# Normalisation on VectorE tile by tile, with mean and root as scalars, in a four-sublayer transformer kernel on one Trainium2 core

## Chip, core and metric

One NeuronCore of a Trainium2 chip runs the whole kernel in one launch. The metric is the device time of that launch in microseconds (us), as the median of several runs. A profiled execution gives the rows shown below.

## What is computed

The input x is 32 sequences of 32 tokens of 128 features (1024 tokens), in float32. Four sublayers are added to it one after the other: an attention behind a language adapter with a layer norm, a low-rank mixture feed-forward, a stack of eight linear-attention blocks, and a routed tree feed-forward with attention. The change bears on the layer norms: one in the first sublayer and two in each of the eight blocks of the third:

```python
def _ln(x, scale, bias):
    m = jnp.mean(x, axis=-1, keepdims=True)
    v = jnp.var(x, axis=-1, keepdims=True)
    return (x - m) * jax.lax.rsqrt(v + EPS_LN) * scale + bias

for i in range(8):
    residual = x
    Q = fmap(x @ Wq[i] + bq[i]); K = fmap(x @ Wk[i] + bk[i]); value = x @ Wv[i] + bv[i]
    KV = einsum('nsh,nsh->nh', K, value); Ksum = sum(K, axis=1)
    V = Q * KV[:, None, :] * 1.0 / (Q * Ksum[:, None, :] + 1e-6)
    x = _ln(gelu(V @ Wo[i] + bo[i]) + residual, ln1_s[i], ln1_b[i])
    residual = x
    x = _ln(gelu(gelu(x @ W1[i] + b1[i]) @ W2[i] + b2[i]) + residual, ln2_s[i], ln2_b[i])
```

## The kernel before

Each engine has an instruction stream written out by hand, and the engines meet only through semaphores. The 1024 tokens are two halves (h = 0, 1) of 512. A half in token order is one SBUF tile of 128 partitions by 512 columns, which are four 128x128 tiles (`TILES` = 4) side by side: token on the partition, feature along the row. `yt[:, h]` is such a half before the norm and `xn[:, h]` after it.

The norm of one half is made by three pieces:

- `stats` (lines 834 to 844) on VectorE (DVE): for each of the four tiles a `bn_stats` (L837) and a `bn_aggr` (L841) leave mean and variance of every token in `mv[:, h, i, 0]` and `mv[:, h, i, 1]`. L843 adds epsilon into `rv` and raises the semaphore `var`. L844 then subtracts the four means from all 512 columns of `yt` in place.
- `root` (L505, L506) on GpSimd (POOL): waits for `var`, raises the 128x4 values of `rv` to the power -0.5 into `rstd`, and raises the semaphore `rstd`.
- `normalise` (lines 846 to 849) on VectorE: waits until its own earlier instructions are written (`own.sync`, L847) and for `rstd` (L848), multiplies all 512 columns of `yt` by the roots into `xn` (L849), and raises `xn`.

Then TensorE (PE) turns the four tiles of `xn` into feature order (L1230), and scale and bias are applied on the way out of PSUM: for the first norm of a block by ScalarE (ACT, L582, function `affine` there), for the second by VectorE (L1122, into `cf`).

The eight blocks are a software pipeline over the halves. One `segment` takes half `a` of block `l` through its attention part and, interleaved, half `b` of block `m` through its feed-forward part. There are 16 segments for VectorE (the first has no second half, twelve are four to each of three passes of a hardware loop), and a last norm stands alone. The order on VectorE within a segment is written out:

```python
def segment(l, a, sa, m, b, sb_):
    keys(l, a, sa)
    values(l, a)
    norm_sum(l, a, 0)          # L831: yt = attention part + residual
    stats(a, EPS_LN)
    if m is not None:
        norm_sum(m, b, 1)      # L831, for the other half
    norm_scale(l, a, 0)        # normalise
    if m is not None:
        stats(b, EPS_LN)
        norm_scale(m, b, 1)    # normalise
        affine(m, b, sb_)      # L1122
```

So there are 34 norms of a half: 2 in the first sublayer and 32 in the blocks (16 of `a`, 15 of `b` and the last one). TensorE waits for each `xn` in its own fixed order, and fills its known gaps with matmuls on a tile of zeros (`keep_warm`, L1237). Near the end POOL has more to do than roots: `split` (L527, L528) divides 128x1024 weights into two parts, a cast followed by a subtraction. One such pair stands in POOL's stream between the last segment's second root and the last root, others right behind the last root. SyncE (SP) issues the weight loads and waits for nothing that the norm makes.

Of the kernel before, what the change touches and what calls it, by code (L numbers as in the profile page):

```python
# [11 lines left out]
ALU = mybir.AluOpType  # L12
# [4 lines left out]
B, S, D = 32, 32, 128  # L17
# [3 lines left out]
TILES = HT // P  # L21
# [125 lines left out]
def network(nc, I, konst, out):  # L147
    ctx = ExitStack()
    with ctx:
        def sb(name, shape, dt=F32):  # L150
            return ctx.enter_context(nc.sbuf_tensor(name, shape, dt))
# [56 lines left out]
        yt = sb("yt", [P, 2, TILES, D])  # L208
        stat = sb("stat", [P, 2, TILES, 6])
        after_stats = sb("after_stats", [P, 1])  # L210
        mv = sb("mv", [P, 2, TILES, 2])
        rv = sb("rv", [P, 2, TILES])
        rstd = sb("rstd", [P, 2, TILES])
# [15 lines left out]
        with ExitStack() as once:  # L229
            def sb_once(name, shape):  # L230
                return once.enter_context(nc.sbuf_tensor(name, shape, F32))
# [4 lines left out]
            xn = sb_once("xn", [P, 2, TILES, D])  # L236
# [33 lines left out]
        S_ = Sems()  # L270
# [27 lines left out]
        def by_batch(ap):  # L298
            return ap.rearrange("p (b s) -> p b s", s=S)
# [8 lines left out]
        def spread(ap, n):  # L308

            return ap.unsqueeze(len(ap.shape)).to_broadcast([*ap.shape, n])  # L310
# [496 lines left out]
        def _(dve):  # L807
            own = Chain(dve, S_["dve"])
            V = nc.vector
# [23 lines left out]
            def stats(h, eps):  # L833

                own.sync()
                for i in range(TILES):
                    own.step(V.bn_stats(stat[:, h, i, :], yt[:, h, i, :]))  # L837
                own.sync()
                own.step(V.memset(after_stats[:, :], 0.0))
                for i in range(TILES):  # L840
                    own.step(V.bn_aggr(mv[:, h, i, :], stat[:, h, i, :]))  # L841
                own.sync()
                V.tensor_scalar(rv[:, h, :], mv[:, h, :, 1], eps, None, ALU.add).then_inc(S_["var"], 1)  # L843
                own.step(V.tensor_tensor(yt[:, h], yt[:, h], spread(mv[:, h, :, 0], D), ALU.subtract))  # L844

            def normalise(n, h):
                own.sync()  # L847
                dve.wait_ge(S_["rstd"], n)  # L848
                V.tensor_tensor(xn[:, h], yt[:, h], spread(rstd[:, h, :], D), ALU.mult).then_inc(S_["xn"], 1)  # L849


            for c in range(LCH):
# [14 lines left out]
            for h in HALVES:  # L867
                dve.wait_ge(S_["a_out"], h + 1)
                add_residual(h, ps[h][:, 3, :], xt[0][:, h].rearrange("p i d -> p (i d)"))
                stats(h, EPS_COND)  # L870
            for h in HALVES:
                normalise(h + 1, h)
# [13 lines left out]
            for h in HALVES:  # L886
                dve.wait_ge(S_["b_qk"], h + 1)
                qe = z(h, 8, 4).rearrange("p g (b j s) -> p (g b) j s", b=GB, j=HPQ)
                for j in range(HPQ):
                    ins = V.tensor_scalar(qe[:, :, j, :], by_batch(ps[h][:, 0, :]), rope_bias[:, 0:1],  # L890
                                          kc[:, K_HEAD + j:K_HEAD + j + 1], ALU.add, ALU.mult)
# [238 lines left out]
            def norm_scale(l, h, n):  # L1130

                normalise(norm_count(l, h, n) + 2, h)
# [4 lines that stand above are left out]
                norm_sum(l, a, 0)  # L1137
                stats(a, EPS_LN)
                if m is not None:
                    norm_sum(m, b, 1)  # L1140
                norm_scale(l, a, 0)
                if m is not None:
                    stats(b, EPS_LN)
                    norm_scale(m, b, 1)
                    affine(m, b, sb_)
# [59 lines left out]
            for h in HALVES:  # L1205
# [5 lines left out]
                for q in range(P // QUAD):  # L1211
                    rows_q = slice(q * QUAD, (q + 1) * QUAD)
                    pt = z(h, 12).rearrange("p (i n) -> p i n", i=TILES)
                    ins = V.transpose(pt[rows_q, :, rows_q], e[rows_q])
# [551 lines left out]
```

## Time and profile before

| | us |
|---|---|
| median of 3 runs | 737.95 (737.72 to 741.58) |
| the profiled execution | 736.44 |
| its span, first to last instruction | 734.5 |
| PE busy in the span | 656.1 |
| VectorE busy | 441.0 |
| ScalarE busy | 309.5 |
| GpSimd busy | 114.2 |

The 1.94 us between the profiled execution and its span lie around the program. The mean TensorE clock granted over the span was 0.943 of full speed. A busy PE includes the matmuls that only fill gaps. The blocks run from about 235 to 560 us.

### The profile page before, as it was taken

How to read it: one execution, taken by the hardware profiler on the slowest of the kernel's cores; microseconds unless marked ns; L12 is line 12 of the kernel's file. 1: busy time of each engine (PE TensorE's matmuls, PEld its weight loads, DVE VectorE, ACT ScalarE, POOL GpSimd, SP SyncE). 2: the span in 40 equal slices, each digit the busy share in tenths (PEclk: the TensorE clock that was granted, in tenths of full speed). 3: DMA queues.
4: the chain of work that ended last, by engine and by line, in shares of the span. 5: the costliest groups of instructions: out<-in, count | busy, mean ns of one | idle time of the engine just before them, and what ended most of it. 6: DMA issues, size and time to landing. Idle time of an engine off the chain costs nothing.

```text
span 734.5 us, 9622 instructions
## 1 busy us (share of the span) xinstructions
PE 656.1 (89%) x3358; PEld 444.6 (61%) x3379; DVE 441.0 (60%) x1021; ACT 309.5 (42%) x488; POOL 114.2 (16%) x93
## 2 busy tenths in 40 slices
PE   9986899899896689999999999999985999999996
PEld 4655586787684345555555555555554877555595
DVE  5579502557768366766666666676655477743344
ACT  4044203343343355555555555555542432344341
POOL 0030130013210011111111111111132127200000
PEclk9599868999999699999999999999996998999997
DMA  3011587000003000101010101010000000000000
GB/s 84 24 44 48 142 222 174 1 0 1 1 0 124 20 1 5 40 1 44 1 43 0 43 0 43 0 43 0 0 1 0 1 1 0 1 0 1 0 1 30
DMA packets 43726, 21.79 MB, mean 30 GB/s; under 512 B 14627, under 2 KB 40799, under 8 KB 43692
## 3 DMA queue, kind: packets, MB, share of 16 engines
q1 hardware_dynamic: 43692, 21.33, 10.8%
q8 instruction: 21, 0.34, 0.2%
q14 instruction: 13, 0.11, 0.0%
HBM read 20.73 MB, written 0.52 MB: 29 GB/s over the span
## 4 chain that ended last, share of the span: by engine, by line
PE 46%; issue 29%; DVE 16%; POOL 5%; ACT 2%; POOLq 0%; DVEq 0%
PE ps L1503 7%; PE ps L1486 7%; POOL rstd L506 5%; PE ps L1692 5%; PE ps L1710 4%; PE ps L1237 3%; PE ps L1716 2%; DVE z L1017 2%; PE ps L1230 2%; PE ps L1283 2%; DVE zr L1058 2%; PE ps L1364 1%; PE ps L1404 1%; PE ps L1377 1%; PE ps L1570 1%
## 5 line engine op out<-in xcount | busy, mean ns | idle before, releaser
L506 POOL TENSOR_TENSOR rstd<-rv,minus_half 128x4 f32<-128x4 f32 x34 | 46.8, 1376 | 334.8 <-DVE rv L843 334.8
L1058 DVE SCALAR_TENSOR_TENSOR zr<-ps,zr 128x512 fp32r<-128x512 f32 x96 | 64.0, 689 | 50.0 <-ACT zr L674 49.5
L674 ACT ACTIVATE zr<-ps 128x512 fp32r<-128x512 f32 x96 | 57.4, 598 | 80.5 <-PE ps L1486 76.6
L1237 PE MATMUL ps<-filler 128*128 128x512 bf16 x303 | 79.8, 402 | 3.3 <-POOL filler L494 0.9
L1582 PE MATMUL ps<-wl,z 128*128 128x128 f32 x512 | 67.9, 281 | 5.4 <-ACT z L730 5.4
L1570 PE MATMUL ps<-cf,wl 128*128 128x512 f32 x128 | 63.0, 615 | 7.0 <-ACT cf L582 7.0
L1582 PEld LDWEIGHTS ps<-wl,z 128*128 128x128 f32 x512 | 60.6, 191 | 12.0 <-ACT z L730 8.3
L1503 PE MATMUL ps<-zr 128*128 128x512 f32 x192 | 61.5, 402 | 6.3 <-DVE zr L1058 6.3
L1486 PE MATMUL ps<-zr 128*128 128x512 f32 x192 | 62.0, 405 | 1.4 <-DVE zr L999 1.4
L1194 DVE SCALAR_TENSOR_TENSOR z<-z,kc 128x512 f32<-128x512 f32 x48 | 34.5, 751 | 44.5 <-ACT z L791 43.1
L730 ACT ACTIVATE z<-ps,vl 128x512 f32<-128x512 f32 x64 | 43.9, 686 | 25.5 <-PE ps L1570 25.3
L791 ACT ACTIVATE z<-ps,cols 128x512 f32<-128x512 f32 x48 | 32.9, 688 | 48.6 <-PE ps L1692 48.4
L1237 PEld LDWEIGHTS ps<-filler 128*128 128x128 bf16 x324 | 33.1, 104 | 33.2 <-issue 7.6
L1535 PE MATMUL ps<-cf,wl 128*128 128x512 f32 x96 | 45.3, 607 | 6.6 <-DVE cf L1122 6.6
L831 DVE TENSOR_TENSOR yt<-ps,z 128x512 f32<-128x512 f32 x32 | 22.0, 688 | 41.1 <-ACT z L720 34.5
L1570 PEld LDWEIGHTS ps<-cf,wl 128*128 128x128 f32 x128 | 23.4, 194 | 38.1 <-issue 23.0
L1503 PEld LDWEIGHTS ps<-zr 128*128 128x128 f32 x192 | 35.8, 192 | 15.8 <-DVE zr L1058 8.8
L1486 PEld LDWEIGHTS ps<-zr 128*128 128x128 f32 x192 | 37.3, 196 | 10.0 <-issue 2.0
L1486 PE MATMUL ps<-zr,arena_r 128*128 128x512 f32 x96 | 38.9, 405 | 0.0
L1503 PE MATMUL ps<-zr,arena_r 128*128 128x512 f32 x96 | 38.0, 395 | 0.0
L849 DVE TENSOR_TENSOR xn<-yt,rstd 128x512 f32<-128x512 f32 x34 | 25.0, 736 | 21.4 <-POOL rstd L506 21.4
L1230 PE MATMUL ps<-kc,xn 128*128 128x128 f32 x136 | 22.9, 294 | 16.7 <-DVE xn L849 15.6
(255 smaller groups left out, 1126.2 us busy)
## 6 DMA issues: line engine op xcount, KB each, us to landing
wl<-in_L_attn_W SPq DMA_DIRECT2D x16, 256.0 KB
big<-in_L_cond_weight SPq DMA_DIRECT2D x32, 64.0 KB, 1.8
arena<-in_L_cond_expert_wi SPq DMA_DIRECT2D x1, 1024.0 KB, 6.7
arena<-in_L_cond_expert_wo SPq DMA_DIRECT2D x4, 256.0 KB, 7.5
big<-in_L_ffn_q_w SPq DMA_DIRECT2D x2, 512.0 KB, 5.2
big<-in_L_ffn_k_w SPq DMA_DIRECT2D x2, 512.0 KB, 7.2
tree_v<-in_L_ffn_v_w SPq DMA_DIRECT2D x2, 512.0 KB, 7.7
arena<-in_L_cond_share_wi SPq DMA_DIRECT2D x1, 768.0 KB, 7.1
```

Of the source, the lines that this page charges most:

```text
L506: nc.gpsimd.tensor_tensor(rstd[:, half, :], rv[:, half, :], minus_half[:, :], ALU.pow).then_inc(S_["rstd"], 1)
L674: nc.scalar.activation(hidden_part(h, n, 0), ps[h][:, n % 2, :], ACT.Relu).then_inc(S_[k + "_hi"], 1)
L730: nc.scalar.activation(z(h, c), ps[h][:, FFN_BANK[c], :], ACT.Gelu_apprx_tanh, bias=col(V_FF + c, s)).then_inc(S_["f_h"], 1)
L1058: V.scalar_tensor_tensor(hidden_part(h, n, 1), ps[h][:, n % 2, :], 0.0, hidden_part(h, n, 0), ALU.max, ALU.subtract).then_inc(S_[k + "_lo" ...
L1230: ins = T.transpose(dst[:, i * P:(i + 1) * P], s, ident)
L1237: T.matmul(bank, filler[:, :].to_broadcast([P, P]), filler[:, :].to_broadcast([P, HT]), start=True, stop=True)
L1486: ins = T.matmul(ps[h][:, n % 2, :], w_part(f, a)[:, c * P:(c + 1) * P], x_part(h, b), start=(m == 0), stop=(m == 2))
L1503: ins = T.matmul(ps[h][:, 2 + f % 2, :], w_part(f, a)[:, FF + c * P:FF + (c + 1) * P], hidden_part(h, n, b), start=(c == 0 and m == 0), st ...
L1535: T.matmul(ps[h][:, (0, 2, 1)[n], :], wl[s][:, n * D:(n + 1) * D], cf[:, h], start=True, stop=True).then_inc(S_[("f_q", "f_k", "f_v")[n]], 1)
L1570: T.matmul(ps[h][:, FFN_BANK[c], :], wl[s][:, 4 * D + c * P:4 * D + (c + 1) * P], cf[:, h], start=True, stop=True).then_inc(S_["f_w1"], 1)
L1582: ins = T.matmul(ps[h][:, 2, tok(h, i)], z(h, c)[:, tok(h, i)], wl[s][:, 4 * D + FF + c * D:4 * D + FF + (c + 1) * D], start=False, stop=( ...
L1692: ins = T.matmul(ps[h][:, n % 2, :], tree_part(t, a)[:, c * P:(c + 1) * P], (xn_r, xf_r)[b][:, h], start=(m == 0), stop=(m == 2))
```

## The change

L844 and `own.sync` in `normalise` go. The multiplication over 512 columns becomes four VectorE instructions over 128 columns each. Each takes the tile of `yt`, subtracts its mean and multiplies by its root; both are operands of one value per partition, read from `mv` and `rstd`. Only the fourth raises `xn`. `yt` stays uncentred and is not read again before it is rewritten.

```diff
                 V.tensor_scalar(rv[:, h, :], mv[:, h, :, 1], eps, None, ALU.add).then_inc(S_["var"], 1)
-                own.step(V.tensor_tensor(yt[:, h], yt[:, h], spread(mv[:, h, :, 0], D), ALU.subtract))
 
             def normalise(n, h):
-                own.sync()
                 dve.wait_ge(S_["rstd"], n)
-                V.tensor_tensor(xn[:, h], yt[:, h], spread(rstd[:, h, :], D), ALU.mult).then_inc(S_["xn"], 1)
+                for i in range(TILES):
+                    ins = V.tensor_scalar(xn[:, h, i, :], yt[:, h, i, :], mv[:, h, i, 0:1], rstd[:, h, i:i + 1],
+                                          ALU.subtract, ALU.mult)
+                ins.then_inc(S_["xn"], 1)
```

## Rows read from the trace of the kernel before

**Rows 1.** The page's costliest groups: busy us, mean ns | idle before, releaser.
```profile
L506 POOL TENSOR_TENSOR rstd<-rv,minus_half 128x4 f32<-128x4 f32 x34 | 46.8, 1376 | 334.8 <-DVE rv L843 334.8
L849 DVE TENSOR_TENSOR xn<-yt,rstd 128x512 f32<-128x512 f32 x34 | 25.0, 736 | 21.4 <-POOL rstd L506 21.4
```

**Rows 2.** The chain that ended last, in one segment: start us, us, what.
```profile
264.90 1.39 POOL rstd L506
266.38 0.69 DVE xn L849
...
268.56 1.39 POOL rstd L506
...
270.04 0.70 DVE xn L849
```

**Rows 3.** The timeline of a loop segment: start us, us, engine, line, what [idle before].
```profile
303.96 0.68 DVE L844 TENSOR_TENSOR yt<-yt,mv 128x512 f32<-128x512 f32 x1
304.13 1.38 POOL L506 TENSOR_TENSOR rstd<-rv,minus_half 128x4 f32<-128x4 f32 x1 [14.58 <-DVE rv L843]
304.57 0.68 DVE L831 TENSOR_TENSOR yt<-ps,z 128x512 f32<-128x512 f32 x1
305.62 0.69 DVE L849 TENSOR_TENSOR xn<-yt,rstd 128x512 f32<-128x512 f32 x1 [0.36 <-POOL rstd L506]
306.23 0.86 DVE L837 BATCH_NORM_STATS2 stat<-yt 128x6 f32<-128x128 f32 x4
...
307.79 1.38 POOL L506 TENSOR_TENSOR rstd<-rv,minus_half 128x4 f32<-128x4 f32 x1 [2.28 <-DVE rv L843]
...
309.20 0.69 DVE L849 TENSOR_TENSOR xn<-yt,rstd 128x512 f32<-128x512 f32 x1 [0.90 <-POOL rstd L506]
...
323.68 1.38 POOL L506 TENSOR_TENSOR rstd<-rv,minus_half 128x4 f32<-128x4 f32 x1 [14.52 <-DVE rv L843]
```

**Rows 4.** Timeline of the first sublayer: its norms and the turn behind them.
```profile
38.69 0.69 DVE L849 TENSOR_TENSOR xn<-yt,rstd 128x512 f32<-128x512 f32 x1 [0.24 <-POOL rstd L506]
...
42.41 1.03 PE L1230 MATMUL ps<-kc,xn 128*128 128x128 f32 x8
```

**Rows 5.** VectorE's groups with their shapes: busy us, mean ns | idle before.
```profile
L1095 DVE TENSOR_SCALAR z<-z 128x512 f32<-128x512 f32 x16 | 6.7, 417 | 0.0
L890 DVE TENSOR_SCALAR z<-ps,rope_bias,kc 128x512 f32<-128x512 f32 x8 | 5.8, 803 | 0.6 <-PE ps L1301 0.6
L823 DVE TENSOR_SCALAR lang_mask<-idf,kc 128x32 f32<-128x32 f32 x3 | 0.5, 222 | 0.0
L826 DVE TENSOR_SCALAR type_mask<-idf 128x32 f32<-128x32 f32 x3 | 0.3, 163 | 0.0
```

**Rows 6.** VectorE's timeline where such instructions follow each other without a wait.
```profile
7.96 0.51 DVE L823 TENSOR_SCALAR lang_mask<-idf,kc 128x32 f32<-128x32 f32 x3
...
46.61 5.84 DVE L890 TENSOR_SCALAR z<-ps,rope_bias,kc 128x512 f32<-128x512 f32 x8 [0.61 <-PE ps L1301]
```

**Rows 7.** The instructions that write or read rstd: min/median/max ns, first and last start.
```profile
L506 POOL TENSOR_TENSOR rstd<-rv,minus_half x34: 1322/1377/1382, 26.9 to 555.7; 128x4 f32<-128x4 f32 x34
```

**Rows 8.** The timeline of the first norm.
```profile
26.66 0.68 DVE L844 TENSOR_TENSOR yt<-yt,mv 128x512 f32<-128x512 f32 x1
26.91 1.32 POOL L506 TENSOR_TENSOR rstd<-rv,minus_half 128x4 f32<-128x4 f32 x1 [24.93 <-DVE rv L843]
```

**Rows 9.** Timeline of a POOL cast that starts under a two-input VectorE instruction.
```profile
608.27 2.14 DVE L1017 TENSOR_TENSOR z<-z,yt 128x512 f32<-128x512 f32 x1
609.81 1.50 POOL L527 CAST arena_r<-big 128x1024 fp32r<-128x1024 f32 x1
```

**Rows 10.** Timeline of the last segment's second norm, beside POOL's split.
```profile
543.72 1.03 POOL L527 CAST zr<-arena 128x1024 fp32r<-128x1024 f32 x1
543.86 1.43 DVE L849 TENSOR_TENSOR xn<-yt,rstd 128x512 f32<-128x512 f32 x1 [0.97 <-POOL rstd L506]
544.83 2.67 POOL L528 TENSOR_TENSOR arena_r<-arena,zr 128x1024 fp32r<-128x1024 f32 x1
```

**Rows 11.** POOL's split line by tile: min/median/max ns, first and last start.
```profile
L528 POOL TENSOR_TENSOR arena_r<-arena,zr x12: 2348/2672/2729, 101.4 to 607.2; 128x1024 fp32r<-128x1024 f32 x12
```

**Rows 12.** Stretches: us, then PE, PEld, DVE, ACT, POOL busy (x), PE clock, DMA share, GB/s.
```profile
255.50:262.30 6.80, 5.46 (x36) 4.05 (x35) 5.04 (x11) 4.03 (x6) 0.00 (x0) 1.00 0.00 0
```

## The prediction

> **What bounds the kernel now.** Start with the page's costliest groups, and look at the idle times. VectorE's L849 waited 21.4 us in all, for the roots alone, and the 34 roots of POOL are long for 512 values: 1376 ns in the mean [rows 1]. The chain that ended last says whether this waiting matters. In one segment of the block pipeline it runs root, `xn` of half `a`, statistics of half `b`, root, `xn` of half `b` [rows 2]. Both roots and both `xn` are on it. So each norm in the blocks is on the path that sets the end, 32 times; a segment lasts 19.55 us (323.68 - 304.13) [rows 3].
>
> The timeline shows where the subtraction L844 stands. It starts at 303.96, before POOL starts its root at 304.13. Behind it L831 ends at 305.25, and VectorE still waits 0.36 us for the root. In half `b` the wait is 0.90 us [rows 3]. The subtraction is thus hidden twice over: nothing of its own 0.68 us stands on the path. The two norms of the first sublayer are on no path at all: the second `xn` ends at 39.38, and TensorE turns it only at 42.41 [rows 4].
>
> **The multiplication becomes four instructions.** No instruction of 128 columns with two scalars from memory is in the trace, so its price is built. From SBUF with constants, the operation took 163 ns at 32 columns and 417 at 512 [rows 5]: 0.53 ns a column, 214 ns at 128. One operand from memory made 163 into 222 ns, thus 59; L890 has two of them and took 803 ns, which is 110 over the 693 of rows 3, about twice 59 [rows 5, 3]. I take 214 + 118 = 332 ns. Started one behind the other, three L823 took 0.51 us together, so they start (0.51 - 0.222)/2 = 0.144 us apart, 0.08 before the end of the one ahead; eight L890 give (5.84 - 0.803)/7 = 0.72, the same 0.08 [rows 5, 6]. Hence 0.252 us from start to start, and 3 x 0.252 + 0.332 = 1.09 us where one instruction took 0.69: **+0.40 us**. The statistics behind it start 4 x 0.252 = 1.01 us after its start, before 0.61 (306.23 - 305.62) [rows 3], again +0.40. Over 32 norms: +12.8 us.
>
> The bounds: if operands from memory cost nothing when instructions follow each other, 3 x 0.134 + 0.214 = 0.62 us, thus -0.075. If the operation loses its fast form with them, the column costs double, 1.06 ns: 803 - 384 x 1.06 = 396 ns, start to start 0.316, together 1.34 us, +0.65. I stay with 0.40, because L823 has the fast form's slope and adds a plain 59 ns, and L890 shows that the additions are not hidden.
>
> **The subtraction releases POOL.** It is hidden, but it may hold up what hides it. In half `a` it ends at 304.64 and the root at 305.51, 0.87 later. In the first norm the root started with 0.43 us of the subtraction left instead of 0.51; it was shorter, 1.32 us, and ended 0.89 after the subtraction (28.23 - 27.34) [rows 3, 8]. The root's length follows the subtraction's end and hardly its own start. Other pairs show why: a POOL cast that takes 1.03 us alone took 1.50 when it started 0.60 before the end of a VectorE instruction with two SBUF inputs [rows 9, 10], 0.47 more, so it lost nothing in its first 0.13 us. L528 took 2.67 instead of 2.35 with 0.46 left of L849 [rows 10, 11]: 0.32 more, so 0.14. So such a POOL instruction needs the way to SBUF about 0.14 us after its start and waits for it. For the root: 0.51 - 0.14 = **0.37 us less**, and 32 x 0.37 = -11.8 us. Bounds: had it needed the way at once, 0.51; had the first root with its 1.32 us been unhindered, only 0.06. I take 0.37, between two pairs that agree; L831, which then overlaps the whole root, has one input in PSUM.
>
> **The wait that goes.** Where two waits stood ahead of L849, it started 0.11 us after the root's end (305.51 to 305.62). In half `b` in the loop it was 0.03 (309.17 to 309.20) [rows 3]. With one wait left I expect 0.03 everywhere: 12 norms (four segments in three passes) have it already, 20 gain 0.07: -1.4 us. Nothing else is queued behind `own.sync`. No DMA, no SP wait and no semaphore of POOL moves with the change.
>
> **The last two norms.** There POOL's split runs beside `xn`. The cast starts at 543.72, L849 at 543.86, and L849 ends only at 545.29, 0.54 after the cast: it waited for it. The subtraction of the split (from 544.83) then waited for L849 [rows 10]. Four instructions leave gaps. The first reads from 544.75 and is through by 544.83, the second by about 545.09, and by then POOL has been asking since 544.97 (0.14 after its start). If it gets in there, it holds until 545.09 + 2.21 = 547.30, and `xn` is ready at 547.6 instead of 545.3: 1.95 us each beyond the 0.40, +3.9 for both; the last norm has the same pair behind its root, and TensorE waits for both. If it does not get in, the four end 0.3 after the old end, 0.1 under the 0.40 each: -0.2. No row shows a VectorE instruction with one input holding the way. The Trainium skill does say so (SBUF — State Buffer, section "Who interferes with whom"): a `tensor_scalar` in a two-port mode and a GpSimd instruction exclude each other, and whichever issues first has the pair for its whole length. By it the break-in is possible, since the third of the four would be issued after POOL's.
>
> **The sum.** +12.8 - 11.8 - 1.4 + 3.9 = +3.5 us. The profiled execution of 736.44 us (span 734.5, and 1.9 around it) would become 739.9; the median of the runs was 737.95, 1.5 above it, so I forecast **741.4 us**. A measurement of this kernel can tell about 0.5% from no change, 3.7 us: between 734.3 and 741.6 nothing is told. The forecast lies just inside, at +0.46%.
>
> **Rivals.**
> - *No break-in* (24%). VectorE keeps the way over its four instructions. 12.8 - 0.2 - 11.8 - 1.4 = -0.6: 737.3 us. For it: the next of the four starts 0.08 before the one ahead ends. Against it: in rows 10 the way went each time to the engine that had asked first, and POOL asks before the third of the four.
> - *The root stays as long as it is* (18%), slower. Place: the 32 roots in the blocks. The first root's 1.32 us would be its free length, and its end 0.02 further behind the subtraction than elsewhere fits that [rows 7, 8]. Price: -1.9 instead of -11.8, thus +9.5, 747.4 us, or with the break-in 751.3. It decides where a root gives back less than 0.36 us with the break-in (15.3 - 32 x 0.36 = 3.8), or 0.24 without. Against it: both other pairs say 0.14.
> - *The fast form is lost* (8%). 30 x 0.65 = 19.5; the last two no longer need the shared way and end 0.1 earlier each; with -11.8 and -1.4, +6.1: 744.1 us.
> - *Operands from memory are free in a row* (10%), faster. Price 32 x -0.075 = -2.4, with -11.8 and -1.4, -15.6: 722.4 us, with the break-in 726.3. Against it stand both start-to-start times of rows 6. The Trainium skill (Vector Engine (DVE) Microarchitecture Reference, section "Measured stream behaviour on trn2") gives about 75 ns an instruction beside the columns and names no price for such operands; an estimate from that page is 4 x (75 + 67) = 567 ns a norm, a gain as well.
> - *Something else, slower* (4%): TensorE's clock falling to its 1.2 GHz level somewhere in the blocks. A stretch with PE busy 5.46 of 6.80 us kept the full 2.4 GHz [rows 12], and my segment stays at 19.5 us, so its gaps hardly grow.
>
> **How the numbers follow.** The forecast has 36%. Its own range is 739.5 to 743.3, from 0.06 us more or less per root. The range 734 to 751 takes in the forecast, no break-in, the lost fast form and the lower half of the unshortened root; the fast rival (10%) and the other half (9%) are left out. Half of the forecast's case lies over 741.6 us. Slower by over 0.5%: 18 + 18 + 8 + 4 = 48%. Within: 18 + 23 = 41%. Faster: 10 + 1 = 11%.
>
> **What the profile of the changed kernel would show.** L844 is gone; four TENSOR_SCALAR of 128x128 in its norm have a mean near 332 ns, and the statistics follow 1.01 us after the first. The roots have a median of 1.0 us instead of 1.377 (of 1.32, if the third case holds). VectorE's wait for the root is about 0.2 us in half `a`, 1.2 in half `b`. The segment is 19.5 us; 20.2 would say that the roots kept their length, 20.0 that the columns cost double, 18.6 that the operands are free. In the last two norms `xn` is ready some 2.3 us later after the cast's end than before, and L528 begins and ends inside the four. I would be wrong if the roots stay above 1.25 us, or if the four take less than 0.9 or more than 1.25 us.

## The result, and the profile after

Over 20 runs of each kernel, the changed one took 743.09 us in the median (739.01 to 747.01) and the one before 736.23. The ratio is 1.0073, with a 95% interval of 1.0054 to 1.0091, so the change costs 4.0 to 6.7 us; the two medians stand 6.9 us apart, just beyond that. Single executions of some kernels ran to between 999 and 2174 us, far above all others of the same kernel; they are in none of the ratios. The changed kernel's profiled execution took 741.60 us with a span of 739.8; before these were 736.44 and 734.5.

**Roots and normalisations.** First the page's costliest groups of the changed kernel (busy us, mean ns | idle before, releaser):

```profile
L506 POOL TENSOR_TENSOR rstd<-rv,minus_half 128x4 f32<-128x4 f32 x34 | 34.3, 1009 | 350.8 <-DVE rv L843 350.8
...
L848 DVE TENSOR_SCALAR xn<-yt,mv,rstd 128x128 f32<-128x128 f32 x136 | 43.6, 383 | 22.8 <-POOL rstd L506 22.7
```

The 34 roots fell from 1376 to 1009 ns [rows 1]: 12.5 us of busy time less. The normalisation rose from 25.0 to 43.6 us. Its mean of 383 ns mixes two things, which the instructions that write or read `rstd` tell apart (min/median/max ns, first and last start):

```profile
L848 DVE TENSOR_SCALAR xn<-yt,mv,rstd x136: 334/341/2501, 36.9 to 562.8; 128x128 f32<-128x128 f32 x136
L506 POOL TENSOR_TENSOR rstd<-rv,minus_half x34: 1007/1008/1038, 26.8 to 558.1; 128x4 f32<-128x4 f32 x34
```

Half of the 136 take 334 to 341 ns, and a few are long, up to 2501. The roots are short everywhere, where before none was under 1322 [rows 7].

**A segment** of the hardware loop, on the timeline of the changed kernel:

```profile
302.36 1.01 POOL L506 TENSOR_TENSOR rstd<-rv,minus_half 128x4 f32<-128x4 f32 x1 [14.94 <-DVE rv L843]
...
302.42 0.69 DVE L831 TENSOR_TENSOR yt<-ps,z 128x512 f32<-128x512 f32 x1
303.41 1.11 DVE L848 TENSOR_SCALAR xn<-yt,mv,rstd 128x128 f32<-128x128 f32 x4 [0.30 <-POOL rstd L506]
304.44 0.86 DVE L837 BATCH_NORM_STATS2 stat<-yt 128x6 f32<-128x128 f32 x4
...
306.00 1.01 POOL L506 TENSOR_TENSOR rstd<-rv,minus_half 128x4 f32<-128x4 f32 x1 [2.63 <-DVE rv L843]
307.05 1.11 DVE L848 TENSOR_SCALAR xn<-yt,mv,rstd 128x128 f32<-128x128 f32 x4 [1.12 <-POOL rstd L506]
...
321.94 1.01 POOL L506 TENSOR_TENSOR rstd<-rv,minus_half 128x4 f32<-128x4 f32 x1 [14.93 <-DVE rv L843]
```

Set it beside [rows 3]. The root ends at 303.37 and `xn` starts at 303.41 in half `a`, 0.04 later, where it was 0.11. The four instructions take 1.11 us instead of 0.69, and the statistics start 1.03 us after the first of them instead of 0.61. The segment is 321.94 - 302.36 = 19.58 us, before 19.55. Two gains and one loss nearly cancel: 2 x 0.42 - 2 x 0.37 - 0.07 = +0.03.

**The loss is at the end of the blocks.** The third root, the first in the blocks, started at 244.61 before and at 242.93 after. The last one started at 555.72 before, 558.14 after:

```profile
242.93 1.01 POOL L506 TENSOR_TENSOR rstd<-rv,minus_half 128x4 f32<-128x4 f32 x1 [36.18 <-DVE rv L843]
...
558.14 1.01 POOL L506 TENSOR_TENSOR rstd<-rv,minus_half 128x4 f32<-128x4 f32 x1 [12.71 <-DVE rv L843]
```

The stretch between grew from 311.1 to 315.2 us, by 4.1, of which the segments explain 15 x 0.03 = 0.5. The rest arises between 541 and 550 us, beside POOL's split. The timeline of the changed kernel there; the same place before is [rows 10]:

```profile
541.97 1.04 POOL L527 CAST zr<-arena 128x1024 fp32r<-128x1024 f32 x1
542.05 3.97 DVE L848 TENSOR_SCALAR xn<-yt,mv,rstd 128x128 f32<-128x128 f32 x4 [1.12 <-POOL rstd L506]
...
543.08 2.34 POOL L528 TENSOR_TENSOR arena_r<-arena,zr 128x1024 fp32r<-128x1024 f32 x1
...
546.08 0.71 PE L1231 MATMUL ps<-kc,xn 128*128 128x128 f32 x4 [2.99 <-DVE xn L848]
...
546.57 3.57 PE L1571 MATMUL ps<-cf,wl 128*128 128x512 f32 x4
```

The four normalisations span 3.97 us, before the one took 1.43. The first of them waits for POOL's cast. To see what the others wait for, the same tile in two shorter windows, 542.0 to 543.0 and 543.0 to 545.4 (busy us, mean ns | idle before):

```profile
L848 DVE TENSOR_SCALAR xn<-yt,mv,rstd 128x128 f32<-128x128 f32 x1 | 1.0, 1035 | 1.1 <-POOL rstd L506 1.1
...
L848 DVE TENSOR_SCALAR xn<-yt,mv,rstd 128x128 f32<-128x128 f32 x2 | 3.5, 1768 | 1.1 <-POOL rstd L506 1.1
```

Two together take 2 x 1768 = 3536 ns, so the second takes 2501. It is recorded from 543.01 to 545.51 (two starts of 0.256 us before the end of all four at 546.02), and L528 runs from 543.08 to 545.42 within it, at 2.34 us, free of any hindrance (before it had 2.67). POOL broke in between the first and the second of the four. `xn` is ready 2.48 us later behind its root than before (4.01 against 1.53). The last norm shows the same 3.97 us.

TensorE then stood idle for 2.99 us and what followed was slow. Before, the timeline had there:

```profile
545.35 0.66 PE L1230 MATMUL ps<-kc,xn 128*128 128x128 f32 x4 [0.89 <-DVE xn L849]
...
545.84 1.88 PE L1570 MATMUL ps<-cf,wl 128*128 128x512 f32 x4
```

The granted clock says why the four matmuls were slow. The stretches 545 to 549 of before, and 545 to 549 and 546.55 to 549.96 of after (columns as in [rows 12]: us, then PE, PEld, DVE, ACT, POOL busy, granted clock):

```profile
545.00:549.00 4.00, 3.65 (x18) 2.25 (x19) 1.10 (x2) 1.56 (x3) 2.50 (x1) 1.00 0.00 0
```
```profile
545.00:549.00 4.00, 2.92 (x7) 1.51 (x8) 1.83 (x4) 0.47 (x1) 0.42 (x1) 0.69 0.00 0
546.55:549.96 3.41, 3.41 (x6) 1.26 (x5) 0.81 (x1) 0.69 (x1) 0.00 (x0) 0.50 0.00 0
```

The clock was granted at half, 1.2 GHz, for 3.4 us right behind the gap. The four matmuls took 3.57 us, before 1.88: +1.7 us. The gap alone does not settle this. The kernel with the one-input cover of experiment 1 has the same break-in and, at the same place, the same gap of 2.99 us, and there the clock stayed at full speed (timeline, and the stretch 540 to 550):

```profile
548.97 0.65 PE L1233 MATMUL ps<-kc,xn 128*128 128x128 f32 x4 [2.99 <-DVE xn L850]
549.46 1.88 PE L1573 MATMUL ps<-cf,wl 128*128 128x512 f32 x4
```
```profile
540.00:550.00 10.00, 5.83 (x24) 2.69 (x23) 8.53 (x23) 2.33 (x4) 5.35 (x4) 1.00 0.00 0
```

The kernel with the two-input cover kept 1.00 behind a gap of 3.36 us. So the 1.7 us belong to the profiled execution of the changed kernel; how often its other executions pay them is not shown.

**The account.** In the blocks: 0.5 from the segments, 2.48 - 0.42 = 2.06 from the first break-in beyond the 0.42 that every norm pays, and 1.7 from the clock make 4.3; the trace has 4.1. Behind the last root the tail grew from 178.8 to 181.6 us, of which the second break-in, less the shorter root, is 2.48 - 0.37 = 2.1; I assign nothing to the other 0.7; the two executions have their stretches at 1.2 GHz at different places there (from 614 to 620 us the mean granted clock was 0.51 before and 1.00 after, from 673 to 676 it was 1.00 before and 0.50 after). The changed execution came to the blocks 1.7 us earlier; the change touches two norms there, off the path, and the granted clock differs there too (0.52 before and 0.60 after between 30 and 40 us, 1.00 and 0.85 between 130 and 140). I take both as scatter. Single executions differ by more: of the 20 executions of the changed kernel the three with a mean granted clock of 0.953 took 739.0 to 739.4 us, the seven with 0.936 to 0.940 took 745.2 to 747.0. 4.1 + 2.9 - 1.7 = 5.3 us, the difference of the spans.

### The profile page after: what moved, and what is told of

The parts are those of the page before. It is cut to its first block, busy times and chain, and to the rows that moved or that the text cites. A ratio compares the mean times of both kernels' runs of the same rounds, so it can differ in the third digit from the quotient of the medians.

```text
span 739.8 us, 9677 instructions
## 1 busy us (share of the span) xinstructions
PE 657.6 (89%) x3379; PEld 442.8 (60%) x3379; DVE 443.9 (60%) x1089; ACT 309.6 (42%) x488; POOL 101.2 (14%) x93
## 4 chain that ended last, share of the span: by engine, by line
PE 43%; issue 30%; DVE 19%; POOL 4%; ACT 2%; SPq 0%; DMA 0%; POOLq 0%; DVEq 0%
PE ps L1504 6%; PE ps L1487 6%; PE ps L1693 5%; POOL rstd L506 4%; PE ps L1711 4%; DVE zr L1059 2%; PE ps L1238 2%; PE ps L1717 2%; DVE z L1018 2%; PE ps L1284 2%; DVE xn L848 2%; PE ps L1231 2%; PE ps L1571 1%; PE ps L1378 1%; PE ps L1405 1%
## 5 line engine op out<-in xcount | busy, mean ns | idle before, releaser
L1238 PE MATMUL ps<-filler 128*128 128x512 bf16 x324 | 82.7, 394 | 1.2 <-POOL filler L494 0.9
L506 POOL TENSOR_TENSOR rstd<-rv,minus_half 128x4 f32<-128x4 f32 x34 | 34.3, 1009 | 350.8 <-DVE rv L843 350.8
L1571 PE MATMUL ps<-cf,wl 128*128 128x512 f32 x128 | 64.7, 629 | 7.0 <-ACT cf L582 7.0
L848 DVE TENSOR_SCALAR xn<-yt,mv,rstd 128x128 f32<-128x128 f32 x136 | 43.6, 383 | 22.8 <-POOL rstd L506 22.7
L1536 PE MATMUL ps<-cf,wl 128*128 128x512 f32 x96 | 45.3, 607 | 6.6 <-DVE cf L1123 6.6
L831 DVE TENSOR_TENSOR yt<-ps,z 128x512 f32<-128x512 f32 x32 | 22.1, 692 | 45.7 <-ACT z L720 34.6
L1231 PEld LDWEIGHTS ps<-kc,xn 128*128 128x128 f32 x136 | 14.9, 145 | 41.7 <-DVE xn L848 40.8
L1487 PE MATMUL ps<-zr,arena_r 128*128 128x512 f32 x96 | 38.4, 400 | 0.0
```

Of the source, the lines that this page charges most:

```text
L506: nc.gpsimd.tensor_tensor(rstd[:, half, :], rv[:, half, :], minus_half[:, :], ALU.pow).then_inc(S_["rstd"], 1)
L848: ins = V.tensor_scalar(xn[:, h, i, :], yt[:, h, i, :], mv[:, h, i, 0:1], rstd[:, h, i:i + 1], ALU.subtract, ALU.mult)
L1231: ins = T.transpose(dst[:, i * P:(i + 1) * P], s, ident)
L1238: T.matmul(bank, filler[:, :].to_broadcast([P, P]), filler[:, :].to_broadcast([P, HT]), start=True, stop=True)
L1487: ins = T.matmul(ps[h][:, n % 2, :], w_part(f, a)[:, c * P:(c + 1) * P], x_part(h, b), start=(m == 0), stop=(m == 2))
L1536: T.matmul(ps[h][:, (0, 2, 1)[n], :], wl[s][:, n * D:(n + 1) * D], cf[:, h], start=True, stop=True).then_inc(S_[("f_q", "f_k", "f_v")[n]], 1)
```

## The experiments

Six questions, eight kernels. Each line number counts in its own kernel.

### 1. Is it the subtraction's second SBUF input that makes the root long?

Two kernels put a VectorE instruction of about 0.68 us back where L844 was. I call it the cover of the root. One cover reads two operands from SBUF (`yt` and the means), the other reads one. The result is used by nobody.

```diff
+                own.step(V.tensor_tensor(xn[:, h], yt[:, h], spread(mv[:, h, :, 0], D), ALU.subtract))
...
             def normalise(n, h):
+                own.sync()
```

> The changed kernel, with the subtraction put back in its old place in the root's shadow (its result goes to xn and is overwritten), and own.sync back. Its result is not needed, so only what it does to POOL can cost. Theory (a VectorE instruction with two SBUF inputs keeps POOL from SBUF until it ends): the roots go from 1.01 back to 1.38 us, a segment from 19.58 to 20.39 us (two roots of 0.37 and one wait of 0.07), the kernel about 13 us over the changed one (743.1), 756. Rival (the roots are shorter for another reason, such as the missing write of yt or fewer semaphores): roots 1.01, a segment 19.65, the kernel 744.5.

```diff
+                own.step(V.tensor_reduce(stat[:, h, :, 0], yt[:, h], AX_X, ALU.add))
...
             def normalise(n, h):
+                own.sync()
```

> The same, but in the root's shadow stands a reduction over the same 512 columns of yt, of about the same length (0.64 to 0.68 us) and with one SBUF input. Theory: POOL is not held up, roots 1.01 us, a segment 19.65, the kernel about 1.4 us over the changed one, 744.5. Rival (any VectorE work on SBUF beside the root lengthens it): roots 1.38, a segment 20.39, 756.

The instructions at `rstd`, of the kernel with two inputs and of that with one:

```profile
L506 POOL TENSOR_TENSOR rstd<-rv,minus_half x34: 1322/1377/1448, 26.9 to 570.6; 128x4 f32<-128x4 f32 x34
```
```profile
L506 POOL TENSOR_TENSOR rstd<-rv,minus_half x34: 1007/1007/1024, 26.9 to 559.3; 128x4 f32<-128x4 f32 x34
```

The two timelines show that the covers stand at the same place, 0.17 us ahead of the root, and are equally long:

```profile
305.78 0.68 DVE L844 TENSOR_TENSOR xn<-yt,mv 128x512 f32<-128x512 f32 x1
305.95 1.38 POOL L506 TENSOR_TENSOR rstd<-rv,minus_half 128x4 f32<-128x4 f32 x1 [15.02 <-DVE rv L843]
```
```profile
303.74 0.68 DVE L844 TENSOR_REDUCE stat<-yt 128x4 f32<-128x512 f32 x1
303.91 1.01 POOL L506 TENSOR_TENSOR rstd<-rv,minus_half 128x4 f32<-128x4 f32 x1 [15.01 <-DVE rv L843]
```

1377 against 1007 ns: that VectorE is busy beside the root costs nothing, and 0.37 us comes with the instruction that reads two operands from SBUF. The covers differ in what they write too, 512 columns against 4; that is not the cause, since in the changed kernel L831 writes 512 columns to SBUF beside each root of half `a`, and that root takes 1.01 us. (Experiment 6 runs the subtraction itself with one SBUF input.) It is paid in full: the segment is 20.40 us with two inputs and 19.69 with one, 0.71 apart for two roots. Over the whole program the first has ratio 1.0312 (1.0215 to 1.0408; three executions, 753.98, 754.99 and 763.83 us), the second 1.012 (1.0086 to 1.0153). Against the changed kernel the one-input kernel loses 0.10 us a segment, all of it in half `a` (3.74 us from root to root, in the changed kernel 3.64). There the root ends at 304.92, but the cover has pushed L831 back to 305.01, and the product follows only then:

```profile
304.33 0.68 DVE L831 TENSOR_TENSOR yt<-ps,z 128x512 f32<-128x512 f32 x1
305.05 1.11 DVE L850 TENSOR_SCALAR xn<-yt,mv,rstd 128x128 f32<-128x128 f32 x4
```

So a root that short no longer hides 0.68 us of cover in full. The two runs refute the rival in which the roots stay long, and confirm the price of the root.

### 2. What does the root alone give, without four instructions?

The kernel before, with the subtraction taken out. It leaves out the subtraction of the mean.

```diff
-                own.step(V.tensor_tensor(yt[:, h], yt[:, h], spread(mv[:, h, :, 0], D), ALU.subtract))
```

> The kernel before, without the subtraction L844 and nothing else changed; the mean is not subtracted. Theory: roots 1.01 us, a segment from 19.55 to 18.81 us, the kernel 11.8 us under the one before: 724.4 if that is 736.2. Rival (the subtraction was hidden and held up nothing): a segment 19.55, the kernel 736. A second rival (its own time was partly on the path as well): a segment under 18.7.

Measured: ratio 0.9876 (0.9821 to 0.993), some 9 us of gain where 11.8 were expected. In the profiled execution the blocks took 311.1 - 301.2 = 9.9 us less; they began 3.6 us later than in the kernel before (248.24 against 244.61), in a part that differs by two norms off the path, and I take that as scatter. The roots are at 1008 ns in the median; the longest, 1393 ns, is the second of the first sublayer, which runs beside the other half's two-input product L848. The segment is 18.88 us, so 0.67 less instead of the 0.74 that two roots give. Where the rest went is on this kernel's timeline, in half `b`:

```profile
309.95 1.98 PE L1569 MATMUL ps<-cf,wl 128*128 128x512 f32 x4 [0.43 <-ACT cf L582]
310.89 0.69 DVE L848 TENSOR_TENSOR xn<-yt,rstd 128x512 f32<-128x512 f32 x1 [1.12 <-POOL rstd L506]
...
311.77 0.60 PE L1229 MATMUL ps<-kc,xn 128*128 128x128 f32 x4
```

`xn` is written at 311.58. TensorE turns it only at 311.77, and no wait stands at the turn: it is still busy with the four matmuls ahead. From the root of `a` to that of `b` the whole 0.38 us arrived (3.28 us, before 3.66), from there to the next segment only 0.29 (15.60, before 15.89). TensorE's own queue is the next thing late.

### 3. What do the operands from memory cost?

The changed kernel with constants in place of the two operands. It leaves out the normalisation.

```diff
-                    ins = V.tensor_scalar(xn[:, h, i, :], yt[:, h, i, :], mv[:, h, i, 0:1], rstd[:, h, i:i + 1],
+                    ins = V.tensor_scalar(xn[:, h, i, :], yt[:, h, i, :], 0.0, 1.0,
```

> The changed kernel, with the constants 0 and 1 in place of mean and root in the four instructions; the normalisation is left out. Theory (each operand from memory costs 59 ns, also from start to start): the four start 0.134 to 0.14 us apart and take 0.62 to 0.63 us together instead of 1.115, a segment 18.6 us, the kernel about 16 us under the changed one: 727. Rival (the price is that of four instructions instead of one, the operands are nearly free): they stay near 0.25 us apart, a segment 19.5, the kernel 742.

The normalisation's line and one place on the timeline:

```profile
L848 DVE TENSOR_SCALAR xn<-yt x136: 214/222/2366, 36.9 to 553.9; 128x128 f32<-128x128 f32 x136
...
309.73 0.64 DVE L848 TENSOR_SCALAR xn<-yt 128x128 f32<-128x128 f32 x4 [1.12 <-POOL rstd L506]
```

Each instruction takes 214 ns against 334, and the four 0.64 us against 1.11. So an operand costs 60 ns in the duration, and (1.11 - 0.64)/4 = 0.12 us for two also from start to start: nothing of it is hidden behind the instruction ahead. The segment is 18.81 us, 0.77 less than the changed kernel's instead of 2 x 0.47, with the turn of half `b` late by TensorE's matmuls as in experiment 2 (0.29 us after `xn` is written). Ratio 0.991 (0.9881 to 0.9939). With free operands the change would have been a gain; the maximum of 2366 ns shows that the break-in is still there and does not hang on the operands.

### 4. What do the break-ins cost?

The changed kernel, with POOL waiting for `xn` before each of the two splits, and the same wait put into the kernel before.

```diff
+            pool.wait_ge(S_["xn"], norm_count(last, 0, 1) + 2)
...
+            pool.wait_ge(S_["xn"], norm_count(last, 1, 1) + 2)
```

> The changed kernel, in which POOL waits for the xn of the last segment's second norm, and for the last xn, before it starts its splits. Theory (POOL's split breaks in among the four instructions): xn takes 1.11 us from its first start instead of 3.97 in both norms, TensorE's clock does not fall in the gap, and the kernel loses 2 x 2.86 + 1.7 = 7.4 us against the changed one: 735.7 if that is 743.1. Rival (what the late split loses comes back as TensorE waiting for its weights): 743.

> The kernel before with the same two waits of POOL. Theory: L849 of the last two norms takes 0.69 us instead of 1.43, the kernel 1.5 us less than before: 734.7 if that is 736.2; so with the collision gone on both sides the change costs 1.0 us (32 x 0.03). Rival: the change costs the same 5 to 7 us with and without the collision.

The changed kernel with the wait, at the place of the first break-in:

```profile
542.62 1.01 POOL L506 TENSOR_TENSOR rstd<-rv,minus_half 128x4 f32<-128x4 f32 x1 [2.63 <-DVE rv L845]
543.66 1.11 DVE L850 TENSOR_SCALAR xn<-yt,mv,rstd 128x128 f32<-128x128 f32 x4 [1.12 <-POOL rstd L506]
544.90 1.04 POOL L527 CAST zr<-arena 128x1024 fp32r<-128x1024 f32 x1 [1.28 <-DVE xn L850]
546.02 2.35 POOL L528 TENSOR_TENSOR arena_r<-arena,zr 128x1024 fp32r<-128x1024 f32 x1
```

Both long norms are gone, 1.11 instead of 3.97 us, and the split is merely later. The stretch in the blocks fell from 315.2 to 310.7 us, with the segment unchanged at 19.58. The ratio is 0.9989 (0.9961 to 1.0017), against 1.0073 of the changed kernel: 0.0084, or 6.2 us for two waits in POOL's stream (expected were 7.4, with 1.7 of clock in them; the intervals leave 2 to 3 us open). A wait of TensorE for the later weights that would take this back does not show, which refutes the rival. Without the break-ins the change is worth nothing either way: beside the kernel before with the same waits, 0.998 (0.9957 to 1.0004), it is 0.0009 or 0.7 us slower, and the two intervals overlap. The loss of the change thus hangs on two norms of 34, as far as intervals of 2 us to either side can tell.

### 5. How much of it is TensorE's clock?

The changed kernel with ten matmuls on the tile of zeros in TensorE's gap ahead of the turn that waits for the first break-in.

```diff
+            keep_warm(10, ps[0][:, 0, :])
```

> The changed kernel with ten filler matmuls (2.2 us) ahead of the turn that waits for the xn that POOL's split delays. Theory (TensorE idles 2.99 us there, its clock falls to 1.2 GHz, and the four matmuls behind it take 3.57 us instead of 1.88): the four take 1.88 us, and the kernel loses 1.7 us: 741.4 if the changed one is 743.1. Rival (they are slow for another reason): no difference, 743.1.

The same stretch of this kernel, in the columns of [rows 12], and its TensorE timeline:

```profile
545.00:549.00 4.00, 3.19 (x17) 2.01 (x17) 1.57 (x4) 1.38 (x2) 0.17 (x1) 1.00 0.00 0
```
```profile
542.67 2.35 PE L1238 MATMUL ps<-filler 128*128 128x512 bf16 x10
545.82 0.66 PE L1231 MATMUL ps<-kc,xn 128*128 128x128 f32 x4 [0.81 <-DVE xn L848]
546.31 1.88 PE L1571 MATMUL ps<-cf,wl 128*128 128x512 f32 x4
```

The idle gap is 0.81 us instead of 2.99, the clock stays at 2.4 GHz, and the four matmuls are back at 1.88 us. The stretch in the blocks is 313.0 instead of 315.2 us; 1.7 of the 2.2 lie behind the last segment's first root (537.11 to 556.19, in the changed kernel 537.37 to 558.14). So the matmuls were slow by the clock and nothing else. That the fillers kept the clock up is not shown: the one-input kernel of experiment 1 kept it without them, over the same gap of 2.99 us, and took about as long there (540.15 to 559.33). In the time of the whole program nothing shows: ratio 1.0065 (1.0035 to 1.0095), against 1.0073. Intervals of 2 us to either side can't tell 1.7 us. The term stands on one profiled execution, and the repeated runs neither show nor refute it.

### 6. Can the kernel before have the short root and keep its single product?

Experiments 1 and 2 say yes, if the subtraction reads only one operand from SBUF. In the 32 norms of the blocks the sum stays in the PSUM bank of its first operand: L831 adds in place there, statistics, subtraction and product read it there.

```diff
             def add_residual(h, src, res, dst):
+                own.step(V.tensor_tensor(dst, src, res, ALU.add))
...
-                add_residual(h, ps[h][:, 3, :], z(h, 4 + n))
+                add_residual(h, ps[h][:, 3, :], z(h, 4 + n), ps[h][:, 3, :])
...
-                own.step(V.tensor_tensor(yt[:, h], yt[:, h], spread(mv[:, h, :, 0], D), ALU.subtract))
+                own.step(V.tensor_tensor(y, y, spread(mv[:, h, :, 0], D), ALU.subtract))
...
+                normalise(norm_count(l, h, n) + 2, h, summed(h))
```

> The kernel before, but in the 32 norms of the blocks the sum with the residual is written back to the PSUM bank that it is read from, and statistics, subtraction and multiplication work on that bank instead of yt. Then subtraction and multiplication have one SBUF input each. Theory: the roots take 1.01 us in spite of the subtraction, and L849 no longer waits for POOL's cast in the last two norms: 11.8 + 1.5 us less than before, 722.9 if that is 736.2, a segment of 18.8 us, and this beats both kernels. Rival (what POOL waits for is any long instruction of VectorE, or reading and writing PSUM costs VectorE more): roots 1.38 us, or a segment of 19.5 us and more, 736 or above.

Its timeline in half `a`, and beside the first split:

```profile
305.68 0.69 DVE L847 TENSOR_TENSOR ps<-ps,mv 128x512 f32<-128x512 f32 x1
305.85 1.01 POOL L506 TENSOR_TENSOR rstd<-rv,minus_half 128x4 f32<-128x4 f32 x1 [14.61 <-DVE rv L846]
306.28 0.69 DVE L831 TENSOR_TENSOR ps<-ps,z 128x512 f32<-128x512 f32 x1
307.00 0.69 DVE L852 TENSOR_TENSOR xn<-ps,rstd 128x512 f32<-128x512 f32 x1
...
537.55 1.04 POOL L527 CAST zr<-arena 128x1024 fp32r<-128x1024 f32 x1
537.70 0.69 DVE L852 TENSOR_TENSOR xn<-ps,rstd 128x512 f32<-128x512 f32 x1 [0.59 <-POOL rstd L506]
```

All 34 roots and all 32 products of the blocks (min/median/max ns, first and last start):

```profile
L506 POOL TENSOR_TENSOR rstd<-rv,minus_half x34: 1007/1008/1384, 26.8 to 548.8; 128x4 f32<-128x4 f32 x34
L852 DVE TENSOR_TENSOR xn<-ps,rstd x32: 692/692/692, 249.4 to 550.0; 128x512 f32<-128x512 f32 x32
```

The subtraction is back in the root's shadow at 0.69 us, and the root takes 1.01 us beside it. Only the two roots of the first sublayer, whose norms stayed in SBUF, are still at 1.32 and 1.38 us. The product starts under the cast and takes 0.69 us, where in [rows 10] it took 1.43: the last two norms are free of the conflict too. The program took 727.17 us in the median of six executions (722.01 to 727.85), ratio 0.9851 (0.9818 to 0.9883): faster than both kernels, by some 11 us against the one before, where 13.3 were expected. The segment is 18.95 us. That is 0.60 less, not the 0.74 of two roots: 0.05 of the missing 0.14 lie between the two roots (3.34 us, before 3.66): the root of half `a` ends at 306.86, but VectorE is busy with L831 until 306.97 and sets the start of the product itself. The other 0.09 lie behind half `b`, where `xn` is written at 310.92 and TensorE turns it at 311.09, late as in experiment 2.

## Why the prediction was right, and where its sum was off

The forecast of 741.4 us lies 1.7 from the measured 743.09, inside the range, and the mechanisms of the product, the root, the wait and the break-in are as they were put. The nearness is in part luck. The change was forecast at +3.5 us, +0.46%, just inside what counts as no change; measured is +0.73%, and 3.5 us lie under the 4.0 where the interval begins. The base made up for it: the forecast stood on 737.95 us, the median of three executions, and the median of 20 is 736.23, so that the same sum would have said 739.7. Slower by over 0.5% had 48%. Of these, 26 stood on two rivals that the runs refute and 4 on the clock, which the trace shows in one execution; only 18 stood on the forecast's own mechanism.

- *The price of the four instructions.* Right in size. Built were 332 ns, 0.252 us from start to start and 1.09 us together; measured 334 to 341 ns, 0.26 and 1.11. The built +0.40 a norm was +0.42; over 32 norms this is +13.4 instead of +12.8 us. Experiment 3 shows the parts too: 214 ns at 128 columns with constants is the number interpolated from rows 5. One support of the sum was weak: L890 reads PSUM, and it was set against 693 ns of another operation, which rows 3 give only as 0.69 us. The estimate of 567 ns for the four is near the 0.64 us with constants and half of what they take with operands from memory. The rivals *operands free in a row* and *fast form lost* are refuted by these numbers.
- *The root.* Right: -0.37 us, in every one of the 34, and experiment 1 shows the cause. The first norm had made the choice hard, with its 1.32 us. At the same place it now takes 1.02, so 0.3 of that were hindrance as well.
- *The wait that goes.* Right: 0.07 us, 0.11 to 0.04 in half `a`.
- *The break-in.* The mechanism was right, with the order off by one: POOL came in before the second of the four, not before the third. The size was nearly met, since the later instructions wait for the same L528 either way: `xn` 2.48 us later behind its root, forecast 1.95 + 0.40 = 2.35. That the second would be through before POOL asked is what failed. The rival *no break-in* is refuted by the trace, and experiment 4 shows that the measured loss goes with the two break-ins, to within its interval.
- *The term left out of the sum* is the clock. "Something else, slower" named TensorE's 1.2 GHz level and was set aside by [rows 12], a stretch with PE busy 5.46 of 6.80 us, because the segment's gaps would hardly grow. That held for the segments. It failed at the one place where the prediction itself lengthened a gap: an idle time of 0.89 us before, with the break-in's 2.35 added and the root's 0.37 taken off, gives a gap of 2.9 us. It was 2.99, and the clock behind it cost 1.7 us in the profiled execution. The step that failed is "my segment stays at 19.5 us, so its gaps hardly grow". What it should have held is a chance of 1.7 us and no fixed term, since the same gap left the clock at full speed in another kernel.
- *The sum.* Measured terms: +13.4 - 11.8 - 1.4 + 2 x 2.06 + 1.7 = +6.0 against +3.5 forecast. The trace shows +5.3, the repeated runs +5.4; the difference lies within the scatter ahead of the blocks and in the tail. Without the clock the measured terms are +4.3.

The Trainium skill (SBUF — State Buffer, section "Who interferes with whom") says that `tensor_scalar` in a two-port mode and a GpSimd instruction exclude each other for the whole length, and that a VectorE instruction with two SBUF inputs contends with a GpSimd instruction that reads SBUF. The trace agrees with both: 1035 ns for a 334 ns instruction under the cast, and experiment 1. Its "whoever issues first" fits less well. The second normalisation is recorded from 543.01, L528 from 543.08, and yet POOL went first. It may be that a VectorE instruction claims the pair only once the one ahead has let go, or only when its own reading begins; no run here separates these from an inexact start in the record.

## What to carry to other kernels

An instruction hidden in another engine's wait can still be what makes that wait long: before you move or drop it, compare the length of what it hides behind with the same instruction elsewhere. Splitting one instruction into several gives another engine a place to break in at every seam; look for each place where a long instruction of the other engine is queued, and order the two by a wait if the split can be later. When your own sum lengthens a gap of TensorE, look at the clock at that gap, not in the stretch where nothing changes, and carry its fall as a possible cost: it came in one kernel and not in another over the same gap.

## What the runs showed of the hardware that was not expected

- Four VectorE instructions in a row lost the shared way to POOL after the first, though the second was recorded 0.07 us ahead of POOL's. The one overtaken lasted 2501 ns instead of 334. With constants as operands it happened too, up to 2366 ns.
- An idle gap of 2.99 us on TensorE was followed by a stretch at 1.2 GHz in one kernel, and by none in another with the same gap, at the same place between the same matmuls; nor was a gap of 3.36 us in a third.
- A VectorE product with one operand in PSUM and one in SBUF ran at 692 ns beside a POOL cast, the same as alone; with both in SBUF it took 1.43 us [rows 10].
